# Two reorderings in a fused ResNeXt and Swin block kernel: SP's loads, stores and wrapped copies, and the attention output's scaling ahead of the MLP input's norm on DVE

## The reference

```python
# block 1: grouped-convolution bottleneck, written to a scratch tensor in DRAM
h = relu(bn(conv1x1(x)));  h = relu(bn(conv3x3_grouped(h)))
x = relu(bn(conv1x1(h)) + x)
# block 2: shifted 7 x 7 window attention and an MLP
y    = roll(ln(x), (-3, -3))                       # rows and columns wrap round
win  = y in windows of 49 tokens
q, k, v = win @ qkv_w.T                            # 8 heads of 16
attn = softmax(q k.T * scale + bias + mask)
out  = (attn @ v) @ proj_w.T + proj_b              # back in place, rolled by (3, 3)
x    = x + out                                     # x2 below
z    = gelu(ln(x) @ fc1_w.T + fc1_b) @ fc2_w.T + fc2_b
return x + z                                       # y below
```

## Time and profile before

| | |
|---|---|
| three runs | 4832.89, 4834.04, 4839.28 us; median 4834.04 |
| profiled execution | 4831.1 us, of which the trace spans 4829.0 |
| PE busy | 4439.0 us (92%), mean granted clock 0.973 |
| DVE, ACT, POOL busy | 67%, 71%, 46% |

### The profile page before, as it was taken

One profiled execution on the slowest core, in us unless ns is written; L12 is line 12 of the kernel. 1 busy time (PEld: TensorE's weight loads), 2 busy tenths in 40 slices (PEclk: granted clock), 3 DMA queues, 4 the chain that ended last, 5 costly groups with the idle time before them and its releaser, 6 DMA issues.

```text
span 4829.0 us, 192181 instructions
## 1 busy us (share of the span) xinstructions
PE 4439.0 (92%) x71190; PEld 3280.4 (68%) x71190; DVE 3214.6 (67%) x7717; ACT 3444.2 (71%) x5644; POOL 2213.1 (46%) x3242
## 2 busy tenths in 40 slices
PE   8999996999999999999999999999999999999998
PEld 5666665666667666667666666666666666677665
DVE  4343435777777777777777777777777777777775
ACT  3444445777787777777777777777777777787776
POOL 4444433444444444444444444444444444444443
PEclk9999998999999999999999999999999999999999
DMA  4445441011001001000001001010010010000000
GB/s 141 148 146 158 147 137 42 27 28 28 27 27 27 26 27 28 26 27 27 27 27 28 27 27 27 27 27 27 27 28 27 27 28 27 27 27 27 26 27 24
DMA packets 298330, 218.64 MB, mean 45 GB/s; under 512 B 43377, under 2 KB 245518, under 8 KB 298190
## 3 DMA queue, kind: packets, MB, share of 16 engines
q1 hardware_dynamic: 294632, 215.41, 15.3%
q10 hardware_dynamic: 3558, 1.07, 0.1%
HBM read 110.73 MB, written 111.94 MB: 46 GB/s over the span
## 4 chain that ended last, share of the span: by engine, by line
issue 51%; POOL 30%; PE 15%; POOLq 2%; DVE 1%; ACT 0%; DMA 0%; DVEq 0%; ACTq 0%
POOL lnp L1145 15%; POOL sc L1222 12%; PE bank L501 6%; PE bank L514 4%; POOL res L1209 2%; PE bank L479 2%; PE bank L470 2%; POOL lnp L1197 1%; POOLq L1219 0%; PE bank L658 0%; POOLq L104 0%; POOLq L111 0%; PE bank L577 0%; POOLq L1195 0%; DVE sc L1051 0%
## 5 line engine op out<-in xcount | busy, mean ns | idle before, releaser
L1222 POOL TENSOR_TENSOR sc<-sc,mx 128x784 f32<-128x784 f32 x512 | 780.1, 1524 | 973.8 <-DVE mx L1057 973.8
L1209 POOL TENSOR_TENSOR res<-x,projb 98x512 f32<-98x512 f32 x256 | 327.5, 1279 | 1072.3 <-DVE x L1093 1072.3
L850 ACT ACTIVATE g<-bank,fc1b 128x392 f32<-128x392 f32 x1024 | 560.2, 592 | 244.7 <-PE bank L651 244.6
L658 PE MATMUL bank<-g,fc_sb 128*128 128x392 f32 x2048 | 716.7, 493 | 0.1
L914 DVE BATCH_NORM_STATS2 st<-x 98x6 f32<-98x128 f32 x2048 | 446.5, 281 | 260.7 <-DMA x<-x_scratch 252.0
L1076 DVE SCALAR_TENSOR_TENSOR xn<-x,lnp 98x128 f32<-98x128 f32 x1024 | 292.8, 348 | 446.7 <-POOL lnp L1145 445.8
L600 PEld LDWEIGHTS bank<-ident_sb,sc 128*113 128x113 f32 x4096 | 496.3, 177 | 106.7 <-DVE shared L1027 103.9
L633 PE MATMUL bank<-wproj,ot 128*98 128x128 f32 x2048 | 310.7, 299 | 269.2 <-DVE ot L1064 269.2
L1051 DVE TENSOR_TENSOR sc<-bank,shared 128x392 f32<-128x392 f32 x1024 | 528.3, 558 | 34.0 <-PE bank L587 33.8
L600 PE MATMUL bank<-ident_sb,sc 128*113 128x128 f32 x4096 | 541.6, 275 | 0.0
L577 PE MATMUL bank<-xt,wqkv 128*128 128x392 f32 x1024 | 480.0, 552 | 39.2 <-ACT xt L825 9.9
(11 more groups left out here) (105 smaller groups left out, 8451.2 us busy)
## 6 DMA issues: line engine op xcount, KB each, us to landing
x<-x_scratch SPq DMA_DIRECT2D x768, 49.0 KB
out_x<-y SPq DMA_DIRECT2D x672, 49.0 KB
xc_even<-in_x SPq DMA_DIRECT2D x128, 196.0 KB
shared<-in_x SPq DMA_DIRECT2D x128, 196.0 KB
x_scratch<-xc_even SPq DMA_DIRECT2D x128, 196.0 KB
x_scratch<-shared SPq DMA_DIRECT2D x128, 196.0 KB
x<-x_scratch SPq DMA_DIRECT2D x256, 38.5 KB
out_x<-y SPq DMA_DIRECT2D x224, 38.5 KB
```

The costliest lines, as they stand in the source:

```text
L658: mm = nc.tensor.matmul(RC[:, 0:ST], fc2[:, c, :], g[:, c], start=c == 0, stop=c == HC - 1)
L850: nc.scalar.activation(g[:, j], ring[:, 0:ST], ACT.Gelu, bias=fc1b[:, j:j + 1]).then_inc(out_, 1)
L1222: P.tensor_tensor(out=s_r, in0=s_r, in1=m_r.to_broadcast([128, 2 * HEADS, N]), op=ALU.subtract).then_inc(sub_done, 1)
```

## The change

It has three parts.

1. SP: the load in front of each store is that of one strip later. `LEAD` goes from 5 to 6, so that `load_strip(s + 6)` comes before `store_strip(s)`, where it came behind it. The first store is taken out of the loop, and the loop body turned by one strip.
2. SP: the two copies out of `wrap_dram`, and the wait for the stores they read, are taken out of `store_strip` into `unwrap`, which stands behind the load and the store of the next strip.
3. DVE: `ot_out(t1)` comes before `x2_norm(t2)`.

```diff
-LEAD = 5
+LEAD = 6
...
-                if wraps:
-                    sp.wait_ge(y_out[u], 16 * MOVES * (STRIPS // 2) * (img + 1))
-                    below = WIN - SHIFT
-                    sp.dma_start(out[img, H - below:H], wrap_dram[img, 0:below]).then_inc(wrapped, 16)
-                    sp.dma_start(out[img, 0:SHIFT], wrap_dram[img, below:WIN]).then_inc(wrapped, 16)
+
+            def unwrap(img):
+                u = (STRIPS - 1) % 2
+                sp.wait_ge(y_out[u], 16 * MOVES * (STRIPS // 2) * (img + 1))
+                below = WIN - SHIFT
+                sp.dma_start(out[img, H - below:H], wrap_dram[img, 0:below]).then_inc(wrapped, 16)
+                sp.dma_start(out[img, 0:SHIFT], wrap_dram[img, below:WIN]).then_inc(wrapped, 16)
...
+            load_strip(0, LEAD, LEAD % 2)
+            store_strip(0, 0, 0)
             with sp.Fori(0, B - 1) as img:
-                for s in range(STRIPS):
+                for s in range(1, STRIPS):
                     if s + LEAD < STRIPS:
                         load_strip(img, s + LEAD, (s + LEAD) % 2)
                     else:
                         load_strip(img + 1, s + LEAD - STRIPS, (s + LEAD) % 2)
                     store_strip(img, s, s % 2)
-            for s in range(STRIPS):
+                load_strip(img + 1, LEAD, LEAD % 2)
+                store_strip(img + 1, 0, 0)
+                unwrap(img)
+            for s in range(1, STRIPS):
                 if s + LEAD < STRIPS:
                     load_strip(B - 1, s + LEAD, (s + LEAD) % 2)
                 store_strip(B - 1, s, s % 2)
+            unwrap(B - 1)
...
+                if t1.there():
+                    ot_out(t1)
                 if t2.there():
                     x2_norm(t2)
-                if t1.there():
-                    ot_out(t1)
                 if t3.there():
                     y_sum(t3)
```

## The result

| | us |
|---|---|
| before, 4 runs | 4832.89 to 4839.28, median 4834.6 |
| changed, 4 runs | 4749.85 to 4757.24, median 4754.06 |
| ratio | 0.983, 95% interval 0.981 to 0.985 |

The changed kernel is faster by 80 us, 1.7%. The forecast was 4756 us. Its profiled execution took 4752.94 us.

A forecast was written before the change was run, and what follows sets the result against it. The ring of y, stores, loads, statistics, z and ot was taken to bound the kernel. 248 strips of 15.42 us gave minus 78: 4831.1 to 4753, and 2.9 for the median made 4756 us; range 4720 to 4810.

The forecast's parts named there:

- The ring of y, stores, loads, statistics, z and `ot`: Closed chain over SP and DVE, each step waiting for the one before; its length was the plain strip's 15.07 us.
- The 164 us: Cost of the 31 image ends in the steady part, 5.3 us each, which the SP edits were to remove whole.
- 15.42: New strip in us: reciprocals end 13.05 in, plus 2.20 on DVE, plus 0.17 hand-overs; bounds 15.31 and 15.53.
- the three steps on DVE: ot, z's norm and y one behind the other after the reciprocals: 0.48, 1.04 and 0.68, together 2.20 us.
- The hand-overs: Passages ACT to DVE (0.03 us) and DVE to PE (0.14), together 0.17, between 0.06 and 0.28.
- The second new wait of PE: At PE's transpose of z, waiting for y: some 0.5 us a strip, besides about 0.3 for ot before the projection.
- the minus 78 reckoned: Steady part: 248 strips of 15.42 us, 3824 us, against 3901.8 us before.
- the parts outside: Eight strips outside the steady part: one image end (about minus 1) and the drain (about plus 1).
- PE did not get the whole wait back: Rival: z's transpose on PE need not wait for y, so a strip takes 14.72 us, in all 4582; chance 5%.
- The image ends went: Rival: wrapped stores or copies still delay a load on SP, ends stay at 5.3 us, 4920 us; chance 5%.
- z's norm did not meet POOL: Rival: z's norm on DVE meets POOL's subtraction and takes 2.40 us, 1.28 more a strip, 5073 us; chance 4%.
- The clock stayed at 1.00: Rival: PE's clock drops in its two gaps, costing about 1.9 us in each strip, 5227 us; chance 4%.

The follow-up runs named there:

- kernel 3: The changed kernel, but the wait and the two copies stand directly behind the wrapped strip's store, as in the kernel before: 4760.7 us, ratio 0.983.
- kernel 9: The changed kernel with LEAD back at 5, so only the wait and copies are moved one strip later: 4846.88 us, ratio 1.001.
- kernel 4: The changed kernel with y's sum in front of z's norm on DVE (ot, y, z): 4778.15 us, ratio 0.987.
- experiment 1: The kernel before with only the two SP edits, z's norm still in front of ot on DVE: 4636.45 us, ratio 0.957.
- kernel 8: The kernel before with both SP edits, and the statistics moved from in front of z's norm to behind y's sum: 4621.64 us, ratio 0.955.
- kernel 7: Both SP edits, z's norm directly behind x1's norm on DVE, first exponentials behind yt and reciprocals on ACT, against the kernel before: 4604.25 us, ratio 0.951.

## Why the prediction was right, point by point

**The bound before.** Right. The ring of y, stores, loads, statistics, z and `ot` was what bound a strip: with the SP edits alone (kernel 1) the strip is 14.95 us where a plain one took 15.07, and the image ends vanish.

**Parts 1 and 2.** Right: no wait for a load, and even image ends. The 164 us are what the ends cost before; as an edit, SP's part measures 194 us on the steady stretch with the old order on DVE (3901.8 - 3708.0) and 137 with the new one (3967.2 - 3829.9), because the plain strip has another bound in each. The load starts 2.26 us into the strip for the 2.55 reckoned, and the copies' place costs nothing. I had put the two edits together; kernels 3 and 9, both with the new order on DVE, show that the first does it alone.

**Part 3.** Right in mechanism and size: 15.44 us for 15.42. The reciprocals end 13.05 us in (3021.15 - 3008.10), the three steps on DVE take 2.22 us. The hand-overs sum to 0.19 for 0.17, but their shares are the other way round: 0.14 us from ACT to DVE (I took 0.03 from a single row of the drain) and 0.05 us from DVE to PE (0.14). Two terms were each wrong by about 0.1 us in opposite ways, and that their sum held is luck.

The first of the two rows came from code behind the loop, the second from another pair of instructions. The program's last three strips stand behind its loop, as code of their own. In all fourteen profiles `ot` is followed by the projection after 0.13 us inside the loop and after 0.05 to 0.06 in those last three; from the reciprocals to `ot`, where nothing else holds it up, it is 0.12 to 0.13 inside and 0.03 behind. The kernel before, in the strip of the earlier trace rows, where `ot` ends at 4785.55:

```profile
4785.60 1.12 PE L633 MATMUL bank<-wproj,ot 128*98 128x128 f32 x8 [0.50 <-DVE ot L1064]
```

The trace has the reason beside it, though no run tests it. Inside the loop the awaited semaphore stands on a register instruction, and `ot` (or the projection's weight load) follows about 0.09 us behind this one's start: in the changed kernel L1071 at 3021.20, `ot` at 3021.29. Behind the loop `ot` and the weight load carry the semaphore themselves. So does the transpose that waits for y, inside the loop too, hence its 0.05. The row for a hand-over has to come from the same loop and from a wait that is carried in the same way.

The second new wait of PE is 0.46 us at L567, named in advance as 0.5; the one for `ot` is 0.42 instead of 0.3, by the first hand-over.

**The sum.** 248 strips gave minus 71.9 us (3901.8 to 3829.9) for the minus 78 reckoned, and the parts outside cost some 3 us, where I had zero: the stretch from the clearing to the first y sum took 71.1 us against 70.5, and that from the 249th y sum to the last 96.8 against 94.7. That is minus 69. The medians differ by 80. The rest is not larger than what executions vary by: 14.6 us in the first stage, and 9.3 behind it between the two of the kernel before. So that 4756 met 4754 to 2 us is partly luck; what the prediction can claim is the strip, 0.02 us off, and of that the hand-overs' sum is luck again.

**The rivals.** PE did not get the whole wait back: kernel 4 shows z's norm on the chain, and not y's bank alone. The image ends went. z's norm did not meet POOL (1.13 us). The clock stayed at 1.00 with two waits of 0.42 and 0.46 us a strip; the rule of the Trainium skill's page "TensorE: Matmul & The Clock Gate" on frequent short idles, which I had weighed as a rival, is not borne out here for gaps of this length, in this kernel.

**What the prediction did not ask.** It reckoned the swap against the kernel before and found a gain in sum. Against the SP edits alone the swap is a loss: 122 us on the steady stretch (3708.0 to 3829.9), 124 by the times of kernels 1 and 3, which ran beside each other. The two lists of minus and plus were in the working, 164 us from SP and about 87 us back from DVE (248 x 0.35); it did not say that the second should then be left out. The old order without a load's wait stood in the trace of before already, in the drain, and experiment 1's forecast of 4632 us was read from there.

## What to carry to other kernels

When two edits come together, price each by itself and in both orders: here one brought about 4% and the other gave more than half of it back, and their sum still looked like a success. Before an instruction that another engine waits for is moved forward, ask whether what it overtakes is waited for one step later by the same engine, as z was by PE; follow the waiter's next wait too. Before a queue is filled with copies or stores, ask which of its entries someone waits for soonest, and put that first: with the load ahead, stores and copies behind it cost nothing here. And take the price of a hand-over from the loop that is forecast, not from the code behind it.

## What the runs showed of the hardware

- z's norm, four DVE instructions with two inputs from SBUF, takes 1.13 us alone, 1.85 us when it starts 0.6 us into a POOL subtraction (kernel 1) and 2.40 us when it starts 0.16 us in front of it (kernel 8), while the subtraction takes 1.52, 1.52 and 1.56 us. The statistics, with one input, take 0.86 us beside it. The Trainium skill, "SBUF — State Buffer", section "Who interferes with whom", says that a DVE instruction with two SBUF inputs and a GpSimd instruction that reads SBUF contend for a shared pair of ports, which is an exclusive lock. The rows agree: one of the four instructions is held, and the other three take 0.34 us each, where all four take 0.34 to 0.35 alone. In kernel 1 it is the first (1.06 us), in kernel 8 the second (1.61 us, L1084's longest above), and both end about 0.15 us behind the subtraction's end (3019.96 against 3019.81, 3008.58 against 3008.43).
- A hand-over from one engine to another took 0.12 to 0.13 us where a register instruction in front of the waiting one carries the wait (reciprocals to `ot`, `ot` to the projection, z to the transpose), and 0.03 to 0.06 us where the waiting one carries it itself (y to the transpose; the first two behind the loop). In the changed kernel each of them stays within 0.01 us over the strips from 2000 to 4300 us; the reciprocals to `ot` took up to 0.24 us in kernel 8. In the forecasts for kernels 7 and 8 these prices were nearly the whole error.
- The first stage of one and the same program varied by 14.6 us, 0.3% of the whole, between executions.
